# The order of the first tiles on three engines, W_up split into halves chunk by chunk, and its slots loaded in two transfers

## What is computed

```python
h = jnp.einsum('bsh,bhk->bsk', hidden_states, Wd) + bd[:, None, :]     # 512 -> 256
h = jax.nn.gelu(h, approximate=False)
h = jnp.einsum('bsk,bkh->bsh', h, Wu) + bu[:, None, :]                 # 256 -> 512
h = residual + h
mean = jnp.mean(h, axis=-1, keepdims=True)
var = jnp.mean(jnp.square(h - mean), axis=-1, keepdims=True)
h = (h - mean) * jax.lax.rsqrt(var + LN_EPS)
return h * g[:, None, :] + b[:, None, :]
```

## Time and profile before

| quantity | value |
|---|---|
| median of 3 runs | 140.22 us (139.83 to 140.54) |
| profiled execution, its time | 139.18 us |
| profiled execution, its span | 137.4 us |
| granted TensorE clock, mean | 0.987 |
| PE busy | 126.3 us, 92% of the span |
| DVE busy | 111.1 us, 81% |
| POOL busy | 106.8 us, 78% |
| ACT busy | 84.5 us, 62% |

### The profile page before, as it was taken

The page is one execution under the profiler, slowest core; times in us unless marked ns, Lnnn a source line. Parts: engine busy times, 40 slices in busy tenths (PEclk is TensorE's granted clock), DMA queues, the critical chain, the costliest instruction groups (busy, mean ns, idle before and its releaser), DMA issues.

```text
span 137.4 us, 4048 instructions
## 1 busy us (share of the span) xinstructions
PE 126.3 (92%) x846; PEld 112.4 (82%) x847; DVE 111.1 (81%) x273; ACT 84.5 (62%) x176; POOL 106.8 (78%) x118
## 2 busy tenths in 40 slices
PE   6887799999999999999999999999999999999830
PEld 6785788878899998799999999999999999998610
DVE  1898768668778988889878897889788978887992
ACT  0766578525586669766666666666666666666600
POOL 7002896967878998688888888888888888889960
PEclk9999999999999999999999999999999999999995
DMA  1969899964655555552554554555456633331365
GB/s 41 341 190 289 253 333 284 281 171 129 181 144 192 152 153 142 152 152 50 153 155 153 153 155 153 153 153 153 153 153 153 153 76 79 76 76 38 79 168 178
DMA packets 13201, 21.95 MB, mean 160 GB/s; under 512 B 2297, under 2 KB 3842, under 8 KB 13186
## 3 DMA queue, kind: packets, MB, share of 16 engines
q1 hardware_dynamic: 8802, 15.74, 40.4%
q10 hardware_dynamic: 4384, 6.05, 15.4%
HBM read 13.39 MB, written 8.65 MB: 160 GB/s over the span
## 4 chain that ended last, share of the span: by engine, by line
PE 59%; DVE 11%; POOL 9%; ACT 5%; issue 5%; DMA 4%; POOLq 2%; ACTq 2%; DVEq 1%
PE hg_ps L886 25%; PE y_ps L919 23%; PE xT_ps L872 7%; POOL res L400 6%; PE hg_ps L895 4%; DMA x_sb<-in_x_dram 3%; ACT xT_hi L472 2%; POOL xb L383 2%; DMA itok_all_i<-in_itok_B_dram 2%; DVE r_stats L706 2%; POOLq L213 2%; DVE scaled L727 2%; DVE hb L694 2%; ACT normed L497 2%; DVE res L742 1%
## 5 line engine op out<-in xcount | busy, mean ns | idle before, releaser
L383 POOL TENSOR_TENSOR xb<-x_sb,bu_rows 128x512 f32<-128x512 f32 x33 | 43.6, 1323 | 10.3 <-DVE bu_rows L681 9.7
L400 POOL TENSOR_TENSOR res<-normed,lnb_rows 128x512 f32<-128x512 f32 x31 | 39.7, 1282 | 9.5 <-ACT normed L497 8.7
L477 ACT ACTIVATE g<-hb 128x256 f32<-128x256 f32 x33 | 13.8, 418 | 35.8 <-DVE hb L694 35.8
L706 DVE BATCH_NORM_STATS2 r_stats<-y_ps 128x6 f32<-128x512 f32 x33 | 22.9, 694 | 5.9 <-issue 5.8
L686 DVE TENSOR_TENSOR xT_lo<-xT_ps,xT_hi 128x512 fp32r<-128x512 f32 x33 | 22.7, 689 | 3.4 <-ACT xT_hi L472 3.4
L886 PE MATMUL hg_ps<-wd_hi,xT_hi 128*128 x132 | 24.0, 304 | 1.0 <-issue 0.8
L919 PE MATMUL y_ps<-wu_hi,gT_hi 128*128 x66 | 23.3, 433 | 1.1 <-ACT gT_hi L482 0.9
L727 DVE SCALAR_TENSOR_TENSOR scaled<-y_ps,r_mv,lnw_rows 128x512 f32<-128x512 f32 x31 | 23.0, 743 | 0.4 <-issue 0.4
L389 POOL TENSOR_TENSOR rstd<-var_eps,half_neg 128x1 f32<-128x1 f32 x33 | 18.1, 548 | 5.5 <-DVE var_eps L715 5.3
L497 ACT ACTIVATE normed<-scaled,rstd 128x512 f32<-128x512 f32 x31 | 22.3, 723 | 0.0
L886 PE MATMUL hg_ps<-wd_hi,xT_lo 128*128 x132 | 21.1, 282 | 0.0
(11 more groups left out here) (88 smaller groups left out, 146.9 us busy)
## 6 DMA issues: line engine op xcount, KB each, us to landing
x_sb<-in_x_dram SPq DMA_DIRECT2D x64, 128.0 KB, 2.9
out_dram<-res ACTq DMA_DIRECT2D x33, 128.0 KB, 2.4
out_dram<-res SPq DMA_DIRECT2D x33, 128.0 KB, 2.3
wd<-in_L_cond_W_down_dram ACTq DMA_DIRECT2D x3, 512.0 KB, 4.9
wu<-in_L_cond_W_up_dram SPq DMA_DIRECT2D x3, 512.0 KB, 5.7
lnw_rows<-in_L_cond_ln_w_dram SPq DMA_DIRECT2D x1, 768.0 KB, 8.2
lnb_rows<-in_L_cond_ln_b_dram SPq DMA_DIRECT2D x1, 768.0 KB, 9.4
x_sb<-in_x_dram ACTq DMA_DIRECT2D x2, 128.0 KB, 3.1
```

Of the source, the lines that this page charges most:

```text
L383: pool.tensor_tensor(xb[:, c % DEEP, :], x_sb[:, c % FAR, :], bu_rows[:, ds(e * H, H)], ALU.add).then_inc(xb_ready, 1)
L400: pool.tensor_tensor(res[:, c % FAR, :], normed[:, c % DEEP, :], lnb_rows[:, ds(e * H, H)], ALU.add).then_inc(res_ready, 1)
L706: dve.bn_stats(r_stats[:, c % DEEP, :], y_ps[c % YBANKS][:]).then_inc(stats_ready, 1)
```

## The change

- **Registers.** PE loads the experts of tiles 0 to 2 in one go before its last three warm-up matmuls; before, it loaded them between `transpose_x(1)` and `down(0)` and between `down(0)` and `down(1)`. DVE loads the experts of its first three `down_bias` before the copy of `bu_rows`. `up(0)` needs no register, as its slot is always 0.
- **W_up.** Each slot is loaded in two transfers of 256 KB with a semaphore each, ACT makes the high half in two instructions of 512 columns, and so does whoever makes the low half. Of slot 2 the first chunk's low half stays with POOL and the second chunk's goes to DVE.
- **ACT.** `keep_down_bias(0)` stands between `x_hi(0)` and `x_hi(1)`; `gelu(0)` stands ahead of `wu_high(0)` and `gelu(1)` ahead of `seed(1)` and `wu_high(1)`.
- **PE.** `transpose_g(1)` stands ahead of `down(2)`; in `up(0)` the product with `wu_lo` comes last instead of second.
- **DVE.** The order around the low halves of W_up is new, `down_bias(1)` comes ahead of `g_lo(0)`, and in the repeated steps for t = 3 to 6 `scale` handles tile t - 3 and stands right behind `down_bias(t + 1)`, where it handled t - 2 and stood behind `x_lo(t + 2)`. At t = 6 (`CLOSER`) both places have a `scale`, and from t = 7 on the order is the old one.

The loop bodies, POOL's order apart from the halved instruction, the loads' order and all the arithmetic are the same.

```diff
@@ -248,8 +250,9 @@
-            eng.dma_start(wu[:, slot, :, :], w_up[ds(e, 1), :, :].rearrange("a (c p) n -> p (a c) n", p=P)).then_inc(
-                wu_in[slot], 16)
+            for k in range(KB):
+                part = w_up[ds(e, 1), k * P:(k + 1) * P, :].rearrange("a p n -> p (a n)")
+                eng.dma_start(wu[:, slot, k, :], part).then_inc(wu_in[slot * KB + k], 16)
@@ -257,11 +260,10 @@
-        def w_up_low(eng, slot):
-            part = slice(slot * KB * H, (slot + 1) * KB * H)
-            eng.wait_ge(wu_hi_ready, slot + 1)
-            return eng.tensor_tensor(wu_lo[:, part], wu[:, slot, :, :].rearrange("p c n -> p (c n)"),
-                                     wu_hi[:, part].bitcast(F32), ALU.subtract)
+        def w_up_low(eng, slot, k):
+            part = slice((slot * KB + k) * H, (slot * KB + k + 1) * H)
+            eng.wait_ge(wu_hi_ready, slot * KB + k + 1)
+            return eng.tensor_tensor(wu_lo[:, part], wu[:, slot, k, :], wu_hi[:, part].bitcast(F32), ALU.subtract)
@@ -416,7 +418,7 @@
             add_bias(3, 3)
-            w_up_low(pool, 2).then_inc(wu_lo_last, 1)
+            w_up_low(pool, 2, 0).then_inc(wu_lo_last, 1)
@@ -498,9 +500,10 @@
             def wu_high(slot):
-                act.wait_ge(wu_in[slot], 16)
-                act.copy(wu_hi[:, slot * KB * H:(slot + 1) * KB * H],
-                         wu[:, slot, :, :].rearrange("p c n -> p (c n)")).then_inc(wu_hi_ready, 1)
+                for k in range(KB):
+                    act.wait_ge(wu_in[slot * KB + k], 16)
+                    act.copy(wu_hi[:, (slot * KB + k) * H:(slot * KB + k + 1) * H], wu[:, slot, k, :]).then_inc(
+                        wu_hi_ready, 1)
@@ -531,16 +534,16 @@
             x_hi(0, 0)
+            keep_down_bias(0)
             x_hi(1, 1)
-            for part in range(len(bd_banks)):
-                keep_down_bias(part)
+            keep_down_bias(1)
+            gelu(0, 0)
             wu_high(0)
-            gelu(0, 0)
             g_hi(0, 0)
             x_hi(2, 2)
+            gelu(1, 1)
             seed(1, 1)
             wu_high(1)
-            gelu(1, 1)
             g_hi(1, 1)
@@ -676,6 +679,9 @@
             w_down_low(dve, 2).then_inc(wd_lo_ready, 1)
+            first_regs = [dve.alloc_register(f"first{i}") for i in range(3)]
+            dve.reg_load(first_regs, tile_expert[0:1, 0:3])
+            first_experts = [dve.snap(reg, min_val=0, max_val=E - 1) for reg in first_regs]
@@ -746,61 +752,58 @@
             dve.wait_ge(bd_ready, len(bd_banks))
-            down_bias(0, 0)
+            down_bias(0, 0, first_experts[0])
             dve.wait_ge(xb_ready, 1)
             dve.tensor_copy(y_ps[0][:], xb[:, 0, :]).then_inc(seeded_first, 1)
-            w_up_low(dve, 0).then_inc(wu_lo_ready, 1)
+            w_up_low(dve, 0, 0).then_inc(wu_lo_ready, 1)
+            down_bias(1, 1, first_experts[1])
             g_lo(0, 0)
-            down_bias(1, 1)
+            w_up_low(dve, 0, 1).then_inc(wu_lo_ready, 1)
             x_lo(2, 2)
-            w_up_low(dve, 1).then_inc(wu_lo_ready, 1)
-            down_bias(2, 2)
+            w_up_low(dve, 1, 0).then_inc(wu_lo_ready, 1)
+            w_up_low(dve, 1, 1).then_inc(wu_lo_ready, 1)
+            down_bias(2, 2, first_experts[2])
             g_lo(1, 1)
             x_lo(3, 3)
-
             stats(0, 0)
+            w_up_low(dve, 2, 1).then_inc(wu_lo_ready, 1)
+            g_lo(2, 2)
             dve.wait_ge(stats_ready, 1)
             mean_var(0, 0)
-            g_lo(2, 2)
+            down_bias(3, 3)
             variance(0, 0)
-            down_bias(3, 3)
             stats(1, 1)
...
             variance(1, 1)
-            scale(0, 0)
...
                 down_bias(t + 1, t + 1)
+                if t <= CLOSER:
+                    scale(t - 3, t - 3)
                 mean_var(t - 1, t - 1)
...
                 x_lo(t + 2, t + 2)
-                scale(t - 2, t - 2)
+                if t >= CLOSER:
+                    scale(t - 2, t - 2)
             scale(LATE - 2, LATE - 2)
...
@@ -849,16 +852,14 @@
                 spread_row(y_ps[e], 1, E + 2 * e + 1).then_inc(up_spread, 1)
-            warm_up(WARM_UPS[2], xT_ps[1])
-
             expert_regs = [pe.alloc_register(f"expert{i}") for i in range(2)]
-            next_regs = [pe.alloc_register(f"next_expert{i}") for i in range(2)]
-
-            def experts_from(t, regs=expert_regs):
-
-                pe.reg_load(regs, up_down[0:1, ds(2 * t, 2)])
-                return [pe.snap(reg, min_val=0, max_val=E - 1) for reg in regs]
+            next_regs = [pe.alloc_register(f"next_expert{i}") for i in range(3)]
+
+            def experts_from(t):
+
+                pe.reg_load(expert_regs, up_down[0:1, ds(2 * t, 2)])
+                return [pe.snap(reg, min_val=0, max_val=E - 1) for reg in expert_regs]
@@ -900,18 +901,19 @@
                 if isinstance(t, int) and t < E:
-                    pe.wait_ge(wu_hi_ready, t + 1)
+                    pe.wait_ge(wu_hi_ready, KB * (t + 1))
                 if isinstance(t, int) and t == 0:
...
                 parts = ((gT_hi, wu_hi), (gT_hi, wu_lo), (gT_lo, wu_hi))
-                if isinstance(t, int) and t == E - 1:
+                if isinstance(t, int) and t in (0, E - 1):
                     parts = ((gT_hi, wu_hi), (gT_lo, wu_hi), (gT_hi, wu_lo))
...
                     if w_half is wu_lo and isinstance(t, int) and t < E - 1:
-                        pe.wait_ge(wu_lo_ready, t + 1)
+                        pe.wait_ge(wu_lo_ready, KB * (t + 1))
                     if w_half is wu_lo and isinstance(t, int) and t == E - 1:
+                        pe.wait_ge(wu_lo_ready, KB * E - 1)
                         pe.wait_ge(wu_lo_last, 1)
@@ -922,17 +924,19 @@
             pe.wait_ge(slots_ready, 2)
+            e_first = expert_of(pe, 0)
+            pe.reg_load(next_regs, up_down[0:1, 1:4])
+            e_next, e_up, e_down = [pe.snap(reg, min_val=0, max_val=E - 1) for reg in next_regs]
+            warm_up(WARM_UPS[2], xT_ps[1])
             transpose_x(0, 0)
...
             pe.wait_ge(wd_hi_ready, E)
-            down(0, 0, expert_of(pe, 0))
-            e0, e1 = experts_from(0)
-            e_up, e_down = experts_from(1, next_regs)
+            down(0, 0, e_first)
             pe.wait_ge(bd_ready, len(bd_banks))
-            down(1, 1, e1)
+            down(1, 1, e_next)
             transpose_g(0, 0)
             transpose_x(2, 2)
-            up(0, 0, e0)
+            up(0, 0, 0)
```

More of the change, by code:

```diff
@@ L58, in adapter_program @@
     LATE = 10
+    CLOSER = 6
     WARM_UPS = 10, 4, 3
@@ L157, in adapter_program @@
         wd_in = [sem(f"wd_in{e}") for e in range(E)]
-        wu_in = [sem(f"wu_in{slot}") for slot in range(E)]
+        wu_in = [sem(f"wu_in{part}") for part in range(E * KB)]
         biases_in = sem("biases_in")
@@ L781, in _ @@
                 x_lo(t + 2, t + 2)
-                scale(t - 2, t - 2)
+                if t >= CLOSER:
+                    scale(t - 2, t - 2)
             scale(LATE - 2, LATE - 2)
             def body(t, c):
-                near = experts_near(t) if from_tile(t, 2) else [None] * 4
-                if exists(t - 1):
-                    stats(t - 1, c - 1)
-                if exists(t):
-                    g_lo(t, c)
-                if exists(t - 1):
-                    dve.wait_ge(stats_ready, t)
-                if exists(t + 1):
-                    down_bias(t + 1, c + 1, near[3])
-                if exists(t - 1):
-                    mean_var(t - 1, c - 1)
-                if exists(t - 1):
-                    variance(t - 1, c - 1)
+                near = experts_near(t)
+                stats(t - 1, c - 1)
+                g_lo(t, c)
+                dve.wait_ge(stats_ready, t)
+                down_bias(t + 1, c + 1, near[3])
+                mean_var(t - 1, c - 1)
+                variance(t - 1, c - 1)
                 if exists(t + 2):
                     x_lo(t + 2, c + 2)
-                if exists(t - 1):
-                    scale(t - 1, c - 1, near[1])
+                scale(t - 1, c - 1, near[1])
                 return near[3], near[2]
@@ L944, in body @@
                 up(t, c, e_up)
+            transpose_g(1, 1)
             down(2, 2, e_down)
-            transpose_g(1, 1)
             transpose_x(3, 3)
```

## The result

| | before | after |
|---|---|---|
| median | 140.03 us (4 runs, 138.9 to 140.54) | 137.91 us (4 runs, 137.59 to 138.23) |
| profiled execution, time / span | 139.18 / 137.4 us | 137.71 / 135.9 us |

The ratio of the runs is 0.9898 with a 95% interval from 0.985 to 0.9946, so the change takes off 1.4 us (0.8 to 2.1). The spans differ by 1.5 us. The forecast was 138.2.

The account below looks back on a forecast made before the run. PE was taken as the bound at 3.48 us a tile. An advance of 0.9 by `up(3)`, plus 0.78 + 0.35 + 0.1 - 0.15 at tiles 4 to 6, gave 2.0 off 140.2: 138.2 us, range 137.2 to 139.3.

Parts of the forecast that it names:

- The bound: PE's loop, 3.48 us a tile and untouched: whatever is won by `up(10)` comes out at the end one for one.
- Tiles 4 to 6: DVE's round from `hb(4)`: moved `scale` fills an idle 0.68, round 3.84 to 3.34 us, PE's waits of 0.78 and 0.35 go.
- Two `scale`s at t = 6: DVE at t = 6: one extra `scaled` of 0.74 us once, charged 0.15 (0 to 0.5).
- The two downs: PE between `down(0)` and `down(1)`: register loads moved away, `down(1)` at 14.1, gain 1.1 us (0.8 to 1.3).
- `up(0)` to `up(3)`: PE's start: advance of 0.6 us after `up(0)`, 0.95 at `up(1)`, 0.9 at `up(3)`, with 0.35 charged for DVE held by POOL.
- the 0.36 that I had won for `up(1)`: Wait between `up(0)` and `up(1)`: goes, as `g_hi(1)` and slot 1's chunks are made during `down(2)`; gain 0.35 us.
- the start's term: Everything ahead of `up(3)`: a net advance of 0.9 us out of the 2.0 forecast.
- My own signs: Wrong if `xT_lo`'s wait stays, DVE's `wu_lo` exceeds 1 us per 512 columns, or `transpose_x` 2 or 5 names DMA.
- The rival of the held DVE: Slot 2, ahead of `hb(3)`: POOL holds DVE the full 1.2 us, 0.85 more than charged; 139.4 us, chance 0.07.
- The stall ahead of `up(10)`: Over half of the 0.68 between `up(5)` and `up(10)`: ACT's order there is untouched, so kept whole.
- The later loads: Tile 5's second half: three more SP issues delay it 1.35 to 1.75 us, landing up to 27.7; nothing charged, 0.3 possible.
- My sentence on the median: Whole kernel before: the median of the runs shown, 140.22 us, is 1.0 above the profiled execution's time.

Follow-up runs that it names:

- oldround: Changed kernel with `scale` back at its old place in the repeated steps of the head; ratio 0.9992 to the kernel before.
- beforeround: Kernel before with only the new place of `scale` in the repeated steps of the head; ratio 0.9896.
- regsold: Changed kernel with the register loads back at their old places on PE and DVE; ratio 0.989 to the kernel before.
- joined: Changed kernel with each W_up slot loaded in one 512 KB transfer again, chunk-wise casts kept; ratio 0.9881 to the kernel before.
- again: The changed kernel itself measured once more, unedited; 137.66 us, ratio 0.9886 to the kernel before.
- both: Changed kernel with POOL's add for tile 3 behind DVE's low halves of slots 0 and 1, and slot 2's two chunks on POOL; ratio 0.9901.
- free1: Changed kernel with POOL's adds for tiles 2 and 3 behind DVE's low halves of slots 0 and 1, slot 2 still split; 137.62 us, ratio 0.9866.
- slot2pool: Changed kernel with both chunks of slot 2's low half on POOL; ratio 0.9906 to the kernel before.
- poolwait: Changed kernel with POOL's add for tile 3 waiting for DVE's low halves of slots 0 and 1; ratio 0.9893 to the kernel before.
- free1joined: Changed kernel with POOL's adds for tiles 2 and 3 behind DVE's low halves, and one 512 KB transfer per W_up slot; 136.94 us, ratio 0.9816.
- free: Changed kernel with POOL's adds for tiles 2 and 3 behind DVE's low halves, and both slot 2 chunks on POOL; 137.84 us, ratio 0.9906.

## Why the prediction was right, and where it was not

- **The bound.** Right. PE's loop takes 3.48 us a tile in both kernels, and what was won by `up(10)` came out at the end: 1.49 of the span's 1.5.
- **Tiles 4 to 6.** Right in place, mechanism and size: 3.34 forecast for the round, 3.44 measured (DVE then waits on PE's pace), 1.1 us forecast and 1.2 measured. oldround and beforeround show it from both sides, and this step is the whole gain that was measured. Two `scale`s at t = 6 were charged 0.15 and cost nothing that shows (`up(5)` to `up(10)` 17.93 against 18.08 before).
- **The two downs.** The mechanism is right and the sum mis-sized: the 1.04 between them became 0.08 (2.47 to 1.51 us, by the earlier trace rows and the rows after). But tile 1's input landed 0.77 later than before, so `down(0)` began 0.49 later, and 0.47 instead of 1.1 was left. By regsold nothing of this term reaches `up(1)`, so to pass it on to the sum was wrong.
- **`up(0)` to `up(3)`.** The term that failed in size: 0.9 forecast ahead of `up(3)`, 0.28 measured. I had priced DVE held by POOL at one place, 0.6 us at slot 2. It was there (0.7), but also at slot 1 (1.1), where POOL's add for tile 3 now meets DVE's chunks, and in every run in which POOL's add for tile 2 kept its place in the new order, `up(1)` stood at 21.10 to 21.23, however early `down(0)` or `up(0)` was (16.57 to 17.38). In the profiled execution after, that third place cost little (16.57, 0.76 for 0.68), because `down(0)` was late itself; there the 0.36 that I had won for `up(1)` went inside `up(0)`, which took 1.84 us (17.38 to 19.22) where I had 1.39 and 0.1 of loss: its last product began at 18.64, when DVE's second chunk (17.91 and 0.68) was done. I had walked DVE's queue and POOL's each by itself. Nor is 0.28 a gain that holds: beforeround, with the old start, had `up(3)` at 28.18, earlier than the new start in after, joined, oldround, regsold and again (28.41 to 28.66). By oldround the start's term, 0.9 of my 2.0, is nothing that can be measured, and 0.5 us at the most by its interval.
- **My own signs.** One of the three that I had named for a wrong prediction came true: `wu_lo` on DVE took 1.37 us for 512 columns (23.46). The wait ahead of `xT_lo` was gone, and no `transpose_x` of tile 2 or 5 named DMA. `down(1)`, `up(0)`, `up(3)` and `up(10)` stand 0.4 to 0.7 us behind where I looked for them (14.1, 17.0, 27.9, 53.4).
- **The rival of the held DVE** had the right mechanism and an upper bound of 1.2 us for its one place, which held. What it lacked was the number of places. The rule that I cited, the Trainium skill (SBUF — State Buffer, the reading of the diagram of ports), that such a lock lasts for the whole instruction and holds whichever engine comes second, agrees with the rows after in both directions: DVE's chunk ends 0.54 behind POOL's instruction twice, and POOL's copy of 66 numbers at 16.72, begun beside a chunk, took 0.69 us, 0.23 elsewhere.
- **The stall ahead of `up(10)`.** Kept whole in the forecast, and kept: 4.01 less 3.48 is 0.53, against 0.57 before.
- **The later loads.** Landing of tile 5 forecast at up to 27.7, measured at 27.8, with no wait. It was 0.4 us from being the bound (28.17 less 27.8); in both and free1 it is.
- **The total** is right by 0.3 us on the median (138.2 against 137.91) partly by chance: two errors of opposite sign met. The gain in the profile is 1.5 where I had 2.0. And the 140.22 that I subtracted it from was high: 140.03 with its fourth run, and 139.22 to 139.42 in the later measurements. From there 2.0 would have given 137.2 to 137.4, too low. My sentence on the median standing 1.0 above the profiled time did not hold after, where it is 0.2.

Open: why tile 1's input lands between 11.5 and 12.8 us from one execution to the next, with split and with single transfers. It was not tried apart from other edits. Nor was it settled why the stall ahead of `up(10)` is 0.5 to 0.7 us in most executions, 0.9 in slot2pool and 1.0 in regsold.

## What to carry to other kernels

Find the engine whose round is longer than the bound's work, and look in its timeline for an idle gap that another instruction of the same round can fill: that single move was the whole gain. What is won ahead of such a round is given back in it, and what is won ahead of a point where two engines exclude each other is lost there, so walk the queues of all engines together and test a start's rework with the later limit removed. When an edit moves nothing, pair it with the removal of the next limit before it is dropped: joined and poolwait did nothing measurable against the change, and with each other and tile 2's add moved as well (free1joined) the ratio was 0.9816 against 0.9886 of again, 0.7% less, though their intervals overlap a little. slot2pool's edit did not become worth anything: in free it made PE wait. And ask the trace of such a run what came last at the start that did not move: in both it was already tile 5's input, and the idle gap ahead of `transpose_g(3)` only looked like the cause.
